# Graph attention on one core: value matmuls ahead of the score matmuls in each steady step

## The reference, cut to what matters

```python
h = jnp.maximum(_layernorm(x, axis=-1), 0.0)          # x is (4096, 256)
q = h @ Wq.T + bq
k = h @ Wk.T + bk
v = h @ Wv.T + bv
a = q @ k.T * scale + adj + adj                       # (4096, 4096), scale = 1/16
x = x + jax.nn.softmax(a, axis=-1) @ v
```

## Time and profile before

| | |
|---|---|
| median of 3 runs | 862.66 us (862.32 to 863.13) |
| the profiled execution, its time | 862.07 us |
| its span, first to last instruction | 860.0 us |
| mean granted TensorE clock over the span | 0.988 |
| PE busy | 819.8 us (95%) |
| DVE busy | 592.9 us (69%) |
| POOL busy | 394.8 us (46%) |
| ACT busy | 343.5 us (40%) |

### The profile page before, as it was taken

The page is one execution under the profiler, slowest core; times in us unless marked ns, Lnnn a source line. Parts: engine busy times, 40 slices in busy tenths (PEclk is TensorE's granted clock), DMA queues, the critical chain, the costliest instruction groups (busy, mean ns, idle before and its releaser), DMA issues.

```text
span 860.0 us, 16570 instructions
## 1 busy us (share of the span) xinstructions
PE 819.8 (95%) x6720; PEld 816.4 (95%) x6720; DVE 592.9 (69%) x986; ACT 343.5 (40%) x616; POOL 394.8 (46%) x325
## 2 busy tenths in 40 slices
PE   5766899999999999999999999999999999999998
PEld 4766799999999999999999999999999999999998
DVE  4455586767777776767777776767777677767764
ACT  2221234444434444444434344443444344443455
POOL 4255354452709082543618081634528090725445
PEclk9988899999999999999999999999999999999999
DMA  4225023232324332333323332333323243423200
GB/s 158 85 70 199 10 76 96 89 111 86 113 74 123 99 111 86 98 105 94 111 74 115 95 123 87 110 88 98 104 81 114 84 123 94 116 86 92 82 26 13
DMA packets 43708, 81.68 MB, mean 95 GB/s; under 512 B 4976, under 2 KB 5616, under 8 KB 43632
## 3 DMA queue, kind: packets, MB, share of 16 engines
q1 hardware_dynamic: 43632, 80.63, 31.1%
HBM read 76.42 MB, written 4.19 MB: 94 GB/s over the span
## 4 chain that ended last, share of the span: by engine, by line
PE 90%; POOL 4%; DVE 3%; ACT 1%; issue 1%; DMA 1%; SPq 0%; DVEq 0%; ACTq 0%
PE ps L276 44%; PE ps L362 14%; PE ps L364 14%; PE ps L363 14%; POOL x_rows L236 4%; PE ps L268 1%; DVE stats L481 1%; PE ps L342 1%; POOL rstd L231 1%; DVE ring_a L512 1%; DVE hT L491 1%; DMA x_rows<-in_x 1%; PE ps L349 0%; ACT hT L409 0%; DVE mean_var L484 0%
## 5 line engine op out<-in xcount | busy, mean ns | idle before, releaser
L276 PE MATMUL ps<-qhl,hT 128*128 128x256 f32 x3072 | 409.3, 283 | 0.1
L276 PEld LDWEIGHTS ps<-qhl,hT 128*128 128x128 f32 x3072 | 386.2, 191 | 0.3 <-DVE v L506 0.3
L252 POOL TENSOR_TENSOR ring_a<-ring_a,m_row 128x512 f32<-128x512 f32 x179 | 230.6, 1340 | 276.6 <-ACT m_row L460 276.6
L362 PE MATMUL ps<-v,p_hi 128*128 128x258 f32 x1024 | 291.2, 284 | 1.2 <-DVE x_res L551 1.2
L364 PE MATMUL ps<-v,p_lo 128*128 128x258 f32 x1024 | 288.7, 282 | 0.0
L363 PE MATMUL ps<-v,p_hi 128*128 128x256 f32 x1024 | 288.6, 282 | 0.0
L456 ACT CAST p_hi<-ps 128x512 fp32r<-128x512 f32 x256 | 150.4, 588 | 231.4 <-PE ps L364 229.4
L512 DVE TENSOR_TENSOR ring_a<-ps,ring_a 128x512 f32<-128x512 f32 x179 | 123.6, 690 | 104.3 <-PE ps L276 103.6
L362 PEld LDWEIGHTS ps<-v,p_hi 128*128 128x128 f32 x1024 | 193.9, 189 | 1.5 <-DVE x_res L551 1.4
L364 PEld LDWEIGHTS ps<-v,p_lo 128*128 128x128 f32 x1024 | 194.0, 189 | 0.0
L363 PEld LDWEIGHTS ps<-v,p_hi 128*128 128x128 f32 x1024 | 193.4, 189 | 0.0
(11 more groups left out here) (63 smaller groups left out, 357.9 us busy)
## 6 DMA issues: line engine op xcount, KB each, us to landing
ring_a<-in_adj SPq DMA_DIRECT2D x179, 256.0 KB, 2.6
ring_b<-in_adj SPq DMA_DIRECT2D x77, 256.0 KB, 2.6
x_res<-in_x SPq DMA_DIRECT2D x16, 256.0 KB, 2.9
out<-x_res SPq DMA_DIRECT2D x16, 256.0 KB, 2.0
x_rows<-in_x SPq DMA_DIRECT2D x7, 512.0 KB, 3.7
x_rows<-in_x SPq DMA_DIRECT2D x4, 128.0 KB, 3.2
w_all<-in_w SPq DMA_DIRECT2D x1, 512.0 KB, 4.4
w_all<-in_w SPq DMA_DIRECT2D x1, 256.0 KB, 4.4
```

The lines of the kernel that those rows point to most:

```text
L252: nc.gpsimd.tensor_tensor(slot_tiles(w), slot_tiles(w), m, ALU.subtract).then_inc(s_sub, 1)
L276: last = nc.tensor.matmul(dst, lhs(a, ib), rhs(c, ib), start=(n == 0), stop=(n == 3 * DB - 1))
L362: nc.tensor.matmul(ps[:, O_BANK + i, 0:VW], hi, v[:, n, 0:VW], start=(n == 0), stop=False)
```

## The change

In each step of the steady loop of TensorE the value matmuls of step s-20 are issued first, then the transposes of the maximum (in units 0 and 1), then the score matmuls of step s. The projection of the next queries in unit 8 stays behind the scores and now ends the step. Nothing else is changed: the lists of the other engines, the buffers and the waits are the same.

```diff
             for s in range(FIRST, STEPS + LAG):
                 b, u = s // UNITS, s % UNITS
-                if s < STEPS:
-                    scores(s)
+                if s >= LAG:
+                    weigh_values(s - LAG)
                 if u == 0 and b <= BLOCKS:
                     turn_max(b - 1)
                 if u == 1 and b <= BLOCKS:
                     spread_max(b - 1)
+                if s < STEPS:
+                    scores(s)
                 if u == UNITS // 2 and b + 1 < BLOCKS:
                     project_q(b + 1)
-                if s >= LAG:
-                    weigh_values(s - LAG)
```

## The result

The changed kernel takes 928.08 us (median of 4 runs, 927.48 to 930.06) against 862.75 us of the kernel before beside it: a ratio of 1.076, 95% interval 1.074 to 1.078. The forecast was 918.4 in a range of 908 to 929; the measured time lies at its upper edge, and one of the four runs beyond it. The profiled execution took 927.48 us with a span of 925.7, 65.7 us more than the span before.

What follows compares the result with a forecast made beforehand. TensorE's unbroken chain of matmuls was taken as the bound; 50.1 us of block waits, 4.9 at the loop's start and 0.7 at its end added 55.7 to 862.07, giving 917.8, or 918.4 as a median, range 908 to 929.

Steps and rivals of the forecast that it cites:

- Ordinary steps: Values following the scores that end the step before: no wait, cost nothing, 0.59 us to spare for the low part.
- turn_max: Unit 0: needs the maximum behind the block's last add, with values alone in between; wait 0.25 us.
- spread_max: Unit 1: needs three DVE results behind the add of unit 0, with values alone in between; wait 0.76 us.
- finish: Unit 4: values wait for `finish`, queued in DVE's list behind unit 3's add; wait 1.94 us, 2.04 with restart.
- project_q: Unit 8: the low part is asked for before DVE has written it; wait 0.33 us, 0.43 with restart.
- The maximum of unit 1: DVE's maximum, held until POOL lets go, delays the values: 0.10 us taken; rival, 1.79 us or more: 6.3 us on top.
- The sum of a block: Waits and restarts of turn, spread, unit 1's maximum, `finish` and projection added: 3.58 us per block, 50.1 us over 14 blocks.
- The clock: Rival: the wait at `finish` makes TensorE's clock fall in each of 14 blocks, 24 us more, 942 us; chance 0.08.
- The start of the loop: No values cover the first turn and spread, so the first values start later; cost 4.9 us.
- the end of the loop: One value group less covers the last block's chain of maximum, exponential and low part; between 0 and 1.43, 0.7 us taken.
- The not-slower rival: DVE serves `finish` as soon as the last values are done, so the time stays at about 862 us; chance 0.03.
- The rival that only `finish` costs: The small waits vanish, leaving 34.2 us of loss from `finish` and the loop's start and end: 897 us; chance 0.08.

Runs made afterwards that it cites:

- the kernel with the `finish` wait only: Kernel before with values ahead of the scores in units 3 and 4 alone; 907.26 us, ratio 1.055.
- the transposes made alone: Kernel before with the changed order (values, transposes, scores) in units 15, 0 and 1 alone; 882.89 us, ratio 1.025.
- two executions with their waits at the same moments: Kernel before with values first in units 3 and 4 alone (907.26 us), and that kernel with block 2's projection issued twice (906.55 us).
- the kernel with the longest wait: Kernel with values first in units 3 and 4 alone, plus four more reductions of 256 elements in `finish`, results unused; 920.88 us, ratio 1.069.

## Why the prediction was right, and what it missed

*Ordinary steps* cost nothing, as forecast: they are 2.84 to 2.89 us in both kernels.

*turn_max* 0.25 forecast, 0.25 measured. *spread_max* 0.76 and 0.77. *finish* 1.94 and 1.94 plus the restart. *project_q* 0.33 and 0.33. *The maximum of unit 1*: 1.4 forecast from the let-go 1.14 us behind POOL's start, 1.39 measured; so the rival that POOL holds it for 1.79 again did not come. The Trainium skill (GPSIMD Engine Reference, Key points) says that GpSimd shares its SBUF interfaces with VectorE and contends with VectorE instructions that have two SBUF inputs. The traces agree with it. With both inputs in SBUF the maximum takes 0.68 and 0.69 us while POOL is idle ahead of the loop, and 1.04, 1.39 or 1.79 us by where in a subtraction it starts; with one input in PSUM it takes 0.70 while POOL works. DVE of the changed kernel, before POOL's first subtraction at 119.56 and behind it:

```profile
112.36 0.68 DVE L524 TENSOR_TENSOR acc<-acc,ring_a 128x512 f32<-128x512 f32 x1
...
113.68 0.69 DVE L524 TENSOR_TENSOR acc<-acc,ring_a 128x512 f32<-128x512 f32 x1
...
121.59 1.04 DVE L524 TENSOR_TENSOR ps<-ring_b 128x512 f32<-128x512 f32 x1
```

The experiments support each place: taking `finish` out of its place in the list took 1.74 us off a block, putting the transposes back 0.95, and the two groups made alone gave 2.05 and 1.10.

Three terms were mis-sized; only the clock's was put at nothing where something came.

1. *The sum of a block*, 3.58 forecast, 3.77 measured. The forecast charged the restart of 0.10 us at `finish` and the projection only. It also comes behind the wait of unit 3, and the two groups of transposes take 0.05 us longer each when they had to wait. 14 blocks: 2.7 us.
2. *The clock*, 0 forecast, 4 x 1.55 = 6.2 us measured. The forecast had it as a rival with 0.08 and priced one fall at 1.7 us, near the 1.55. The step that failed is to take "the clock falls" or "it stays" as one case for all 14 waits, by whether 1.94 us is nearer to 1.17 or to 4.2. It fell behind some and not behind others. By the prediction's own signs this is where it was wrong, since it named a fall behind x_res as one; the other two, a wait on x_res under 1.5 us and ordinary steps over 2.9, did not come.
3. *The start of the loop*. The first block lasts 48.98 us from its turn, 6.40 more than before; 0.45 of that is the projection's wait, so 5.95 for 4.9 forecast. The clock fell from 120 to 124 us here (0.60, so 4 x 0.40 = 1.6 us lost); without it 4.35, less than forecast, as the maximum of unit 1 was held only to 1.04 us.

With the end of the loop (about 0.9 for 0.7) they make 52.8 + 6.2 + 5.95 + 0.9 = 65.9 us, for 65.7 in the spans; the first turn comes 0.17 us earlier. That the time still lies in the range is in part luck: nothing in the range was meant for the clock, the 6.3 us kept for POOL's hold were not used, and with the 10 falls of the kernel with the `finish` wait only it would have been 6 x 1.55 = 9.3 us longer, some 937 us. PE's busy time did not stay near 820 us either, as the first section shows. The not-slower rival, that DVE serves `finish` before the add, is refuted by the reciprocal that starts 0.61 us behind the add. The rival that only `finish` costs is refuted by the 1.10 us a block of the transposes made alone. Without the five falls (6.2 and 1.6 us) the changed kernel would stand at 920.3 us, for 918.4 forecast.

## What to carry to other kernels

When a saturated engine's list is reordered, each consumer's list has to be read with it: a result that stood ahead of a wait is now behind it, and here one 1.1 us piece of work cost 2 us in each block because it was queued behind an add of 0.7 us that waited for the newer matmuls. Count from the end of the group that the consumer waits for to the start of the next group that needs anything from behind this wait. Read the loss from start to start: the row of a wait shows only what is idle between modelled ends, and at `finish` the loss was 2.04 us with its restart, for 1.77 in the row. A new wait of 2 us on TensorE can have a second price, its clock, which here was paid in some passes and not in others.

## What the runs showed of the hardware that was not expected

The clock's fall does not go by the length of the wait alone. Waits of 1.94 us from start to start (1.77 in the row) were followed by a fall in 10, 10, 4, 4 and 2 of 14 blocks in five kernels, waits of 1.55 us in none, and waits of about 3.3 us in 4. Within one execution the waits were equal, and some felled the clock and others did not, so something beside the length counts. That this is the moment of the wait is likely but not shown: the only sign is that two executions with their waits at the same moments had the same outcome five times out of the first six. What the moment would be counted against is open, and so is why the kernel with the longest wait spread over 9 us. A fall is not bound to `finish`: with the transposes early the clock also fell at the start of the loop, behind waits of 2.1 and 2.04 us at the first turn and the first spread. One fall cost 1.50 to 1.55 us, read as the difference of two periods of the same kernel.

The Trainium skill (TensorE: Matmul & The Clock Gate, section "HAM oscillation — how this bites in real kernels") describes a loop that pays the fall in every pass, with waits of some 3 to 5 us in each. The traces here, with shorter waits, show a fall in some passes and none in others.
